# The seam between attention and the routed experts: order of the last masks, weights, gathers and attention groups

## The chip, the cores and the metric

One core of one Trainium2 chip. The metric is device time in microseconds of one execution of the whole program; lower is better. The core's engines run their own instruction streams in order and meet at semaphores: TensorE (PE, matmuls), VectorE (DVE), ScalarE (ACT), GpSimd (POOL, which also issues indirect DMAs) and SyncE (SP, which issues plain DMAs). TensorE's clock has two levels, 1.2 and 2.4 GHz; the trace gives the granted share.

## What is computed

x has 4 x 1024 tokens of 256 numbers. xn is its layer norm. The result is x + attention(xn) + experts(xn):

```python
qkv = xn @ w_attn.T                      # 16 heads of 16
# causal linear attention, phi = elu + 1, chunks of 128 tokens with a carried state
scores = where(mask, q_c @ k_c.T, 0)
num = scores @ v_c + q_c @ S;  den = scores.sum(-1) + q_c @ z
S = S + k_c.T @ v_c;           z = z + k_c.sum()
attn = (num / (den + 1e-6)) @ w_proj.T
# 8 experts, each token goes to the one of the largest gate logit
e = argmax(xn @ gate_w.T + gate_b + expert_bias)
ffn = relu(xn @ w1[e] + b1[e]) @ w2[e] + b2[e]
```

## The kernel before

**Attention.** The 4096 tokens are 32 chunks of 128 (NC = 32; 0 to 31). A loop over steps p runs every engine over several chunks at once, in a software pipeline written out by hand: at step p, for instance, TensorE does qk of chunk p - 1, the scores of chunk p - 3 and the projection of chunk p - 4. Products are taken in split precision: an f16 high part and an f16 remainder. For a chunk c the last steps are: scores(c) (TensorE, L466), s_mask(c, 0..3) (VectorE, L785, causal mask out of PSUM), inter(c) and pv(c) (L479, L495), y1(c) (ScalarE copy, L1186), yt1(c) (transposes, L525), y(c) (VectorE, division, L801 to L807), yt2(c) (L531), y2(c) (ScalarE copy, L1192), pr(c) (projection, L539), res(c) (VectorE adds the residual, L813). SyncE stores [f16 parts of xn | sum] of each chunk to scr (store_res, L346), and the f16 parts alone, earlier, to scr16 (store_x16). Chunks 29, 30 and 31 are finished behind the loop, in a hand-written order on each engine.

**Weights.** Beside attention the experts' weights are brought into f16 high and low parts, 64 quarters (NW = 64, n = 0 to 63) of 128x512. For each: load_split(n) on SyncE (L320) into one of four staging buffers, which it may reuse once p_wlo has counted w_lo(n - 4); w_scale(n) and w_hi(n) on ScalarE (L1207, L1199; split(first, n) does n such pairs); w_lo(n) on GpSimd (L1370). Behind the loop SyncE still issues quarters 58 to 63, GpSimd does w_lo(56), km(31), w_lo(57) to w_lo(62), and w_lo(63) behind the first gather; ScalarE does split(56, 1), vh(31), y1(29), split(57, 3), y1(30), y2(29), split(60, 4), y1(31), y2(30).

**Routing.** Every 8 chunks the picked experts are turned into ranks by a scan and two matmuls, place(g) (L551, L552), which wait for the scan (v_ox) and for vh and lg of the chunks so far. Behind the last, place(3), VectorE does bases (L913 to L919: the first slot of each expert), own, own_sum, own_slot, first_slots (L972 to L977, the slot KT of each token), to_slots (L983, L985) and places (L967), which build one-hot matrices. 32 matmuls (L628) of these make the table ids: for each of 39 slots (NS = 39) of 128 places, all of one expert, the tokens in it. GE, ESF, ESP and PKF (L1051 to L1057) give each slot's expert; v_es releases the register loads of TensorE and VectorE.

**Slots.** Per slot s: a gather of the rows (GpSimd, indirect DMA), tx(s) (transposes, L647, and ScalarE copy, L1264), 8 groups g1(s, f) of 6 matmuls (L682), bias, high and low (L1080, L1273, L1092), 8 groups g2 (L695) 12 groups behind g1 (LAG), rest and add_up (L1100 to L1112), scatter (L1433). The first three slots gather f16 rows from scr16 (gather_x16, L1421), which needs only ids; the others take scr (gather, L1428), which needs the stores of the last chunks, chunk 31's among them. The gathers from scr begin with slot 0's, since its residual is needed too, so slot 3's is the fourth. PE's order around the seam:

```python
scores(NC - 2)
st(NC - 2)
place(3)
...
a.then_inc(t_ids, 1)
e.wait_ge(S["t32"], n_state(NC - 2))
inter(NC - 1)
yt1(NC - 2)
pv(NC - 1)
yt2(NC - 2)
pr(NC - 2)
yt1(NC - 1)
```

yt2(31) and pr(31) stand inside slot 0, after its groups 3 and 5.

Of the kernel before, what the change touches and what calls it, by code (L numbers as in the profile page):

```python
# [9 lines left out]
ALU = mybir.AluOpType  # L10
# [58 lines left out]
def program(nc, x, wall, wp, gb, eb, w1, b1, w2, b2, cst, cst2, cst3, tri, out):  # L69
    ctx = ExitStack()  # L70
    with ctx:
# [189 lines left out]
        def experts(engine, tile, unit, s, n):  # L261
# [34 lines left out]
        v_o16, v_ox, t_rk, v_own, v_es, v_eq, v_ao, t_ids, v_ids, d_c16 = (  # L296
            sem(n) for n in ("v_o16", "v_ox", "t_rk", "v_own", "v_es", "v_eq", "v_ao", "t_ids", "v_ids", "d_c16"))
# [83 lines left out]
        def tensor(e):  # L381
# [229 lines left out]

            scores(NC - 2)
            st(NC - 2)
            place(3)
# [19 lines left out]
            yt2(NC - 2)  # L634
            pr(NC - 2)
            yt1(NC - 1)
# [67 lines left out]
            tx(0)  # L704
            for t in range(8 * NS + LAG):
                s, f = t // 8, t % 8
                if s < NS:
                    g1(s, f)
                    if f == 2 and s + 1 < NS:
                        tx(s + 1)  # L710
                    if f == 4 and s + 1 < NS:
                        expert(s + 1)
                if t == 3:
                    yt2(NC - 1)
                if t == 5:
                    pr(NC - 1)
                if t >= LAG:
                    g2((t - LAG) // 8, (t - LAG) % 8)

        def vector(e):  # L720
# [248 lines left out]
            def first_slots():  # L969

                e.wait_ge(v_wmx, NW)
                e.tensor_tensor(RB8, OA, bm(BAS, NC), ALU.mult).then_inc(dv.up(), 1)  # L972
                e.wait_ge(dv.sem, dv.n)
                e.tensor_reduce(OB, RB8, X_AX, ALU.add).then_inc(dv.up(), 1)
                e.wait_ge(dv.sem, dv.n)
                e.wait_ge(p_pl, 3)
                e.tensor_tensor(KT, KS, OB, ALU.add).then_inc(dv.up(), 1)  # L977

            def to_slots(i):

                c = slice(16 * i, 16 * i + 16)
                e.wait_ge(dv.sem, dv.n)
# [57 lines left out]
            res(NC - 3)  # L1040
            e.wait_ge(t_ids, 1)
# [5 lines left out]
            e.scalar_tensor_tensor(ids[:, :], pid, 2048.0, IDP, ALU.add, ALU.subtract).then_inc(v_ids, 1)  # L1047
            s_mask(NC - 1, 1)
            s_mask(NC - 1, 2)
            s_mask(NC - 1, 3)  # L1050
            e.tensor_tensor(GE, bc(cc(C_SL, 5 * NP), 7), bm(CSF[:, 0:7], 5 * NP), ALU.is_ge).then_inc(dv.up(), 1)  # L1051
            e.wait_ge(dv.sem, dv.n)
            e.tensor_reduce(ESF, GE, X_AX, ALU.add).then_inc(dv.up(), 1)
            e.wait_ge(dv.sem, dv.n)
            e.tensor_tensor(ESP, ESF, cc(C_PK, 5 * NP), ALU.mult).then_inc(dv.up(), 1)
            e.wait_ge(dv.sem, dv.n)
            e.tensor_reduce(PKF, ESP.rearrange("p (j i) -> p j i", i=5), X_AX, ALU.add).then_inc(dv.up(), 1)  # L1057
            e.tensor_copy(es[:, :], ESF[:, 0:NS])
            y(NC - 2)
            e.wait_ge(dv.sem, dv.n)  # L1060
            e.tensor_copy(pk[:, :], PKF).then_inc(v_es, 1)
            scales_ffn()
            y(NC - 1)
            res(NC - 2)
# [50 lines left out]
            for s in range(NS + 2):  # L1115
# [5 lines left out]
                if s == 0:  # L1121
                    res(NC - 1)
                if s >= 2:
                    add_up(s - 2)
                if s < NS:
                    low(2 * s)
                    bias(s, 1)
# [5 lines left out]
        def scalar(e):  # L1133
# [120 lines left out]
            y1(NC - 2)  # L1254
            y2(NC - 3)
            split(NW - 4, 4)
# [19 lines left out]
            y2(NC - 1)  # L1276
            for s in range(NS):
                if s + 1 < NS:
                    tx(s + 1)
                high(2 * s)  # L1280
                high(2 * s + 1)

        def gpsimd(e):
# [129 lines left out]
            for n in range(NW - 7, NW - 1):  # L1413
                w_lo(n)
# [22 lines left out]
            gather_x16(0)  # L1437
            w_lo(NW - 1)
            for s in range(1, NX0):
                gather_x16(s)  # L1440
# [73 lines left out]
```

## Time and profile before

| | |
|---|---|
| median of 3 runs | 518.91 us (518.23 to 519.29) |
| the profiled execution, device time | 517.53 us |
| its span, first to last instruction | 515.7 us |
| TensorE (PE) busy | 487.0 us, 94% |
| VectorE (DVE) busy | 394.5 us, 76% |
| ScalarE (ACT) busy | 278.7 us, 54% |
| GpSimd (POOL) busy | 304.1 us, 59% |
| granted TensorE clock, mean | 0.980 |

Attention fills the first 265 us or so, the slots run from 287.6 us on; between them lies the seam that the change is about. Busy times are of an average over stages. Times in the rows are us from the start of the span. "L" numbers are lines of the kernel. In the timeline a line is start, length, engine, line, operation, and in brackets how long the engine idled before it and for what; consecutive instructions of one kind are merged (x16).

### The profile page before, as it was taken

Reading aid. Unit: us, or ns where it says so; the run is one execution under the profiler, and the core shown is the slowest. Engines: PE = TensorE matmul, PEld = TensorE weight load, DVE = VectorE, ACT = ScalarE, POOL = GpSimd, SP = SyncE. Lnnn points to the kernel's source line nnn. Section 1 sums busy time; section 2 is a strip of 40 time slices with the busy share of each in tenths; the row PEclk is TensorE's granted clock in tenths of the full one; section 3 lists DMA queues with packets and bytes.
Section 4 is the critical chain, followed back from the end, with each engine's and each line's share of the span. In section 5 each row is a group of like instructions: output and inputs, shape, how many; then the busy total and the mean of one; then the engine's idle time right before and its main releaser. Section 6 shows DMA issues by size and latency. Waiting matters only on the chain.

```text
span 515.7 us, 17822 instructions
## 1 busy us (share of the span) xinstructions
PE 487.0 (94%) x6225; PEld 402.9 (78%) x6225; DVE 394.5 (76%) x851; ACT 278.7 (54%) x536; POOL 304.1 (59%) x498
## 2 busy tenths in 40 slices
PE   7799999999999999999966969999999999999996
PEld 6678887888878888788845758888888888888884
DVE  3688888988889888897897446776776776777775
ACT  3458788778787778878863213323333333333330
POOL 5666888788888888888646074344344344343122
PEclk9799999999999999999988889999999999999999
DMA  8716667676576667665533162221222212200000
GB/s 262 244 53 177 198 200 208 194 216 209 187 221 178 213 187 222 205 205 169 182 111 111 65 174 73 63 79 59 73 64 65 82 59 62 72 23 26 23 15 3
DMA packets 39059, 67.50 MB, mean 131 GB/s; under 512 B 6237, under 2 KB 14686, under 8 KB 38848
## 3 DMA queue, kind: packets, MB, share of 16 engines
q1 hardware_dynamic: 33840, 53.37, 33.5%
q0 software_dynamic: 5136, 12.99, 8.5%
q8 instruction: 56, 0.92, 0.7%
q14 instruction: 27, 0.22, 0.2%
HBM read 51.39 MB, written 17.69 MB: 134 GB/s over the span
## 4 chain that ended last, share of the span: by engine, by line
PE 86%; DVE 5%; DMA 3%; issue 2%; ACT 1%; POOL 1%; DVEq 0%; POOLq 0%; ACTq 0%
PE ps L682 20%; PE ps L695 19%; PE ps L424 8%; PE ps L539 6%; PE ps L466 6%; PE ps L495 5%; PE ps L479 4%; PE ps L442 4%; PE ps L509 3%; PE ps L525 2%; PE ps L647 2%; PE ps L449 2%; PE ps L531 1%; DMA XR<-scr,AR 1%; PE ps L407 1%
## 5 line engine op out<-in xcount | busy, mean ns | idle before, releaser
L682 PEld LDWEIGHTS ps<-AR,W 128*128 x1872 | 131.5, 98 | 41.1 <-issue 2.0
L682 PE MATMUL ps<-AR,W 128*128 128x128 f16 x1872 | 156.1, 220 | 0.9 <-ACT AR L1264 0.9
L695 PE MATMUL ps<-W,ST 128*128 x624 | 151.4, 328 | 0.0
L1273 ACT ACTIVATE ST<-ST 128x512 f16<-128x512 f32 x78 | 49.2, 630 | 117.4 <-DVE ST L1080 117.4
L1080 DVE SCALAR_TENSOR_TENSOR ST<-ps,TAs,B1S 128x512 f32<-128x512 f32 x78 | 58.6, 751 | 48.5 <-PE ps L682 48.5
L1433 POOL DMA_INDIRECT out<-AR x39 | 39.6, 1015 | 93.9 <-DVE AR L1112 90.6
L785 DVE TENSOR_TENSOR AR<-ps,CT 128x512 f32<-128x512 f32 x128 | 82.0, 683 | 2.0 <-PE ps L466 1.7
L1370 POOL TENSOR_TENSOR W<-ST,W 128x512 f16<-128x512 f32 x64 | 75.1, 1174 | 12.3 <-ACT W L1199 12.0
L1428 POOL DMA_INDIRECT XR<-scr,AR x39 | 44.9, 1151 | 52.6 <-DVE AR L1100 23.8
L1092 DVE SCALAR_TENSOR_TENSOR ST<-ST 128x512 f16<-128x512 f32 x78 | 53.6, 687 | 14.9 <-ACT ST L1273 14.9
L424 PE MATMUL ps<-xT,WA 128*128 128x128 f16 x768 | 49.5, 222 | 3.2 <-ACT xT L1148 3.2
L695 PEld LDWEIGHTS ps<-W,ST 128*128 128x128 f16 x624 | 48.5, 98 | 1.6
L424 PEld LDWEIGHTS ps<-xT,WA 128*128 128x128 f16 x768 | 45.6, 99 | 4.5 <-ACT xT L1148 4.2
L1207 ACT ACTIVATE ST<-ST,SC 128x512 f32<-128x512 f32 x64 | 46.4, 725 | 0.0
L820 DVE TENSOR_REDUCE MX<-ST 128x1 f32<-128x512 f32 x64 | 42.5, 665 | 0.1
L1199 ACT ACTIVATE W<-ST 128x512 f16<-128x512 f32 x64 | 40.4, 631 | 1.1
L1322 POOL TENSOR_SCALAR AR<-XR,mv,rsn 128x256 f32<-128x256 f32 x32 | 39.8, 1243 | 1.7
L1264 ACT ACTIVATE AR<-ps 128x512 f16<-128x512 f16 x39 | 23.3, 596 | 31.9 <-PE ps L647 31.9
L1336 POOL TENSOR_TENSOR AR<-AR,CT 128x512 f32<-128x512 f32 x32 | 33.3, 1040 | 7.6 <-DVE AR L779 7.4
L539 PE MATMUL ps<-AR 128*128 128x256 f32 x128 | 36.8, 412 | 0.9 <-ACT AR L1192 0.9
L466 PE MATMUL ps<-AR 32*128 32x256 f32 x512 | 36.8, 401 | 0.9 <-DVE XR L813 0.9
L495 PE MATMUL ps<-AR 128*32 128x128 f32 x1024 | 34.8, 276 | 0.6 <-DVE AR L785 0.6
(149 smaller groups left out, 786.5 us busy)
## 6 DMA issues: line engine op xcount, KB each, us to landing
ST<-in_w SPq DMA_DIRECT2D x128, 256.0 KB, 4.3
scr<-XR SPq DMA_DIRECT2D x32, 256.0 KB, 2.1
XR<-in_x SPq DMA_DIRECT2D x32, 128.0 KB, 4.7
scr<-XR SPq DMA_DIRECT2D x32, 128.0 KB, 4.5
AR<-in_b SPq DMA_DIRECT2D x1, 1024.0 KB, 5.1
AR<-in_wall SPq DMA_DIRECT2D x2, 388.0 KB, 3.8
XR<-scr,AR POOLq DMA_INDIRECT x40, 3.6
out<-AR POOLq DMA_INDIRECT x39, 2.5
```

The source lines that it names most:

```text
L424: a = e.matmul(PS[0][:, j * 128:(j + 1) * 128], WA[:, wl, k, j * 128:(j + 1) * 128], x_part(c, xl_, k), start=(n == 1), stop=(n == 6))
L466: a = e.matmul(psc(c, r)[:, g * 256:(g + 1) * 256], QK[c % 2][rows, 256 + g * 128:384 + g * 128], QM[c % 2][rows, g], start=True, stop=True)
L495: a = e.matmul(PS[5][32 * b:32 * b + 32, j * 128:(j + 1) * 128], V32[c % 2][:, 8 * g + 4 * i + b, :], S32[2 * i + t][:, (2 * g + o) * 128: ...
L539: a = e.matmul(py(c)[:, 256:512], YT2[:, k * 128:(k + 1) * 128], WPF[:, k, :], start=(k == 0), stop=(k == 1))
L682: a = e.matmul(dst, W[:, off:off + 57472][:, bass.ds(place_of(s), 128)], XT16[s % 2][:, xl * 256 + k * 128:xl * 256 + (k + 1) * 128], star ...
L695: a = e.matmul(PS[4 + s % 2][:, 0:w], src[h % 4][:, fs], W[:, off:off + 57344 + w][:, bass.ds(place_of(s), w)], start=(f == 0 and w == 512 ...
L785: e.tensor_tensor(S32[r].rearrange("p (b n) -> p b n", b=4), psc(c, r)[:, :].rearrange("p (b n) -> p b n", b=4), msk, ALU.mult).then_inc(s ...
L1080: e.scalar_tensor_tensor(H32[h % 2].rearrange("p (f n) -> p f n", f=4), PS[h % 4][:, :].rearrange("p (f n) -> p f n", f=4), TAs[:, :, 0][: ...
L1092: e.scalar_tensor_tensor(HL2[h % 4], H32[h % 2], 0.0, HH[h % 4], ALU.max, ALU.subtract).then_inc(v_hl, 1)
L1207: e.activation(src, src, ACT.Copy, scale=SC[:, n // 8, n % 8 // 4:n % 8 // 4 + 1].bitcast(F32)).then_inc(a_wsc, 1)
L1273: e.activation(HH[h % 4], H32[h % 2], ACT.Relu).then_inc(a_hh, 1)
L1370: e.tensor_tensor(lo_, src, hi, ALU.subtract).then_inc(p_wlo, 1)
```

## The change

- TensorE: place(3) moves ahead of scores(30) and st(30). yt2(30), pr(30) and yt1(31) move from ahead of the first slot to inside slot 0: behind tx(0), behind group 0 and behind group 1. yt2(31) and pr(31) go from behind groups 3 and 5 to behind groups 4 and 6.
- VectorE: KT counts on a semaphore of its own, v_kt. The first three operations of the slots' experts (GE, ESF, ESP) move ahead of the wait for the table, the rest right behind ids, so v_es comes ahead of three of chunk 31's masks and y(30). res(30) goes ahead of y(31); res(31) goes behind low(0).
- ScalarE: quarters 60 and 61 are split ahead of y2(29), 62 and 63 behind it. y2(31) goes behind tx(1).
- GpSimd: a wait for v_kt ahead of w_lo(57); w_lo(63) ahead of the first gather.

```diff
@@ -293,8 +293,8 @@
         v_mx, t_mx, v_mm, t_mxa, v_sc, v_ffn = (sem(n) for n in ("v_mx", "t_mx", "v_mm", "t_mxa", "v_sc", "v_ffn"))
 
         p_tt, p_carry, v_ro, p_pl = (sem(n) for n in ("p_tt", "p_carry", "v_ro", "p_pl"))
-        v_o16, v_ox, t_rk, v_own, v_es, v_eq, v_ao, t_ids, v_ids, d_c16 = (
-            sem(n) for n in ("v_o16", "v_ox", "t_rk", "v_own", "v_es", "v_eq", "v_ao", "t_ids", "v_ids", "d_c16"))
+        v_o16, v_ox, t_rk, v_own, v_es, v_kt, v_eq, v_ao, t_ids, v_ids, d_c16 = (
+            sem(n) for n in ("v_o16", "v_ox", "t_rk", "v_own", "v_es", "v_kt", "v_eq", "v_ao", "t_ids", "v_ids", "d_c16"))
 
         v_rb, t_tx, a_tx, v_out, t_g2 = (sem(f"f_{n}") for n in ("rb", "ptx", "tx", "out", "g2"))
 
@@ -609,9 +609,9 @@
                     e.transpose(PBX, BM[:, :], ID32).then_inc(t_bmx, 1)
 
 
+            place(3)
             scores(NC - 2)
             st(NC - 2)
-            place(3)
             yt1(NC - 3)
             inter(NC - 2)
             pv(NC - 2)
@@ -631,9 +631,6 @@
             inter(NC - 1)
             yt1(NC - 2)
             pv(NC - 1)
-            yt2(NC - 2)
-            pr(NC - 2)
-            yt1(NC - 1)
 
             def tx(s):
 
@@ -702,6 +699,7 @@
             e.wait_ge(v_es, 1)
             expert(0)
             tx(0)
+            yt2(NC - 2)
             for t in range(8 * NS + LAG):
                 s, f = t // 8, t % 8
                 if s < NS:
@@ -710,9 +708,13 @@
                         tx(s + 1)
                     if f == 4 and s + 1 < NS:
                         expert(s + 1)
-                if t == 3:
+                if t == 0:
+                    pr(NC - 2)
+                if t == 1:
+                    yt1(NC - 1)
+                if t == 4:
                     yt2(NC - 1)
-                if t == 5:
+                if t == 6:
                     pr(NC - 1)
                 if t >= LAG:
                     g2((t - LAG) // 8, (t - LAG) % 8)
@@ -974,12 +976,12 @@
                 e.tensor_reduce(OB, RB8, X_AX, ALU.add).then_inc(dv.up(), 1)
                 e.wait_ge(dv.sem, dv.n)
                 e.wait_ge(p_pl, 3)
-                e.tensor_tensor(KT, KS, OB, ALU.add).then_inc(dv.up(), 1)
+                e.tensor_tensor(KT, KS, OB, ALU.add).then_inc(v_kt, 1)
+                e.wait_ge(v_kt, 1)
 
             def to_slots(i):
 
                 c = slice(16 * i, 16 * i + 16)
-                e.wait_ge(dv.sem, dv.n)
                 e.tensor_tensor(EQS[:, :, c], SLX[:, :, c], bm(KT[:, c], NS), ALU.is_equal).then_inc(dv.up(), 1)
                 e.wait_ge(dv.sem, dv.n)
                 e.tensor_tensor(EQS[:, :, c], EQS[:, :, c], bm(IDX[:, c], NS), ALU.mult).then_inc(v_eq, 1)
@@ -1038,6 +1040,11 @@
             places(3)
             s_mask(NC - 1, 0)
             res(NC - 3)
+            e.tensor_tensor(GE, bc(cc(C_SL, 5 * NP), 7), bm(CSF[:, 0:7], 5 * NP), ALU.is_ge).then_inc(dv.up(), 1)
+            e.wait_ge(dv.sem, dv.n)
+            e.tensor_reduce(ESF, GE, X_AX, ALU.add).then_inc(dv.up(), 1)
+            e.wait_ge(dv.sem, dv.n)
+            e.tensor_tensor(ESP, ESF, cc(C_PK, 5 * NP), ALU.mult).then_inc(dv.up(), 1)
             e.wait_ge(t_ids, 1)
             pid = PS[1][:, 0:NS]
             e.tensor_scalar(IDZ, pid, 0.0, 2048.0, ALU.is_equal, ALU.mult).then_inc(dv.up(), 1)
@@ -1045,23 +1052,17 @@
             e.scalar_tensor_tensor(IDP, pid, 0.0, IDZ, ALU.is_gt, ALU.subtract).then_inc(dv.up(), 1)
             e.wait_ge(dv.sem, dv.n)
             e.scalar_tensor_tensor(ids[:, :], pid, 2048.0, IDP, ALU.add, ALU.subtract).then_inc(v_ids, 1)
+            e.tensor_reduce(PKF, ESP.rearrange("p (j i) -> p j i", i=5), X_AX, ALU.add).then_inc(dv.up(), 1)
+            e.tensor_copy(es[:, :], ESF[:, 0:NS])
+            e.wait_ge(dv.sem, dv.n)
+            e.tensor_copy(pk[:, :], PKF).then_inc(v_es, 1)
             s_mask(NC - 1, 1)
             s_mask(NC - 1, 2)
             s_mask(NC - 1, 3)
-            e.tensor_tensor(GE, bc(cc(C_SL, 5 * NP), 7), bm(CSF[:, 0:7], 5 * NP), ALU.is_ge).then_inc(dv.up(), 1)
-            e.wait_ge(dv.sem, dv.n)
-            e.tensor_reduce(ESF, GE, X_AX, ALU.add).then_inc(dv.up(), 1)
-            e.wait_ge(dv.sem, dv.n)
-            e.tensor_tensor(ESP, ESF, cc(C_PK, 5 * NP), ALU.mult).then_inc(dv.up(), 1)
-            e.wait_ge(dv.sem, dv.n)
-            e.tensor_reduce(PKF, ESP.rearrange("p (j i) -> p j i", i=5), X_AX, ALU.add).then_inc(dv.up(), 1)
-            e.tensor_copy(es[:, :], ESF[:, 0:NS])
             y(NC - 2)
-            e.wait_ge(dv.sem, dv.n)
-            e.tensor_copy(pk[:, :], PKF).then_inc(v_es, 1)
             scales_ffn()
+            res(NC - 2)
             y(NC - 1)
-            res(NC - 2)
 
             at = {}
 
@@ -1118,12 +1119,13 @@
                         e.wait_ge(v_es, 1)
                     expert(s)
                     bias(s, 0)
-                if s == 0:
-                    res(NC - 1)
                 if s >= 2:
                     add_up(s - 2)
                 if s < NS:
                     low(2 * s)
+                if s == 0:
+                    res(NC - 1)
+                if s < NS:
                     bias(s, 1)
                 if 1 <= s <= NS:
                     rest(s - 1)
@@ -1252,8 +1254,9 @@
             y1(NC - 3)
             split(NW - 7, 3)
             y1(NC - 2)
+            split(NW - 4, 2)
             y2(NC - 3)
-            split(NW - 4, 4)
+            split(NW - 2, 2)
             y1(NC - 1)
             y2(NC - 2)
 
@@ -1273,10 +1276,11 @@
                 e.activation(HH[h % 4], H32[h % 2], ACT.Relu).then_inc(a_hh, 1)
 
             tx(0)
-            y2(NC - 1)
             for s in range(NS):
                 if s + 1 < NS:
                     tx(s + 1)
+                if s == 0:
+                    y2(NC - 1)
                 high(2 * s)
                 high(2 * s + 1)
 
@@ -1410,7 +1414,8 @@
             e.wait_ge(v_ox, 4)
             w_lo(NW - 8)
             km(NC - 1)
-            for n in range(NW - 7, NW - 1):
+            e.wait_ge(v_kt, 1)
+            for n in range(NW - 7, NW):
                 w_lo(n)
             e.wait_ge(S["xt"], NC)
             for c in range(NC - R, NC):
@@ -1434,9 +1439,7 @@
                                      bounds_check=NT - 1, oob_is_err=False).then_inc(d_sca[s % 3], 16)
 
             e.wait_ge(v_ids, 1)
-            gather_x16(0)
-            w_lo(NW - 1)
-            for s in range(1, NX0):
+            for s in range(NX0):
                 gather_x16(s)
             for c in range(NC - R, NC):
                 e.wait_ge(d_scr[c % R], 16 * (c // R + 1))
```

## Rows read from the trace of the kernel before

**Rows 1.** The chain of waits from 235 us on: start us, length us, what.

```profile
268.92 2.07 PE ps L539 x4
271.00 2.93 PE ps L385 x30
273.93 2.32 PE ps L628 x32
...
292.31 2.00 DMA scr<-XR
...
299.46 3.66 DMA XR<-scr,AR
...
306.03 0.64 PE ps L682 x6
308.18 0.34 PE ps L682 x6
```

**Rows 2.** Windows: us, busy us of each engine, TensorE's granted clock, DMA share, GB/s.

```profile
269.00:270.00 1.00, 1.00 (x3) 0.82 (x4) 0.96 (x3) 0.97 (x2) 0.00 (x0) 0.50 0.00 0
```

**Rows 3.** The timeline from 254.5 to 277 us, all engines.

```profile
258.84 0.46 ACT L1175 ACTIVATE AR<-ps,SV 128x256 f32<-128x256 f32 x1
...
258.91 1.15 PE L466 MATMUL ps<-AR 32*128 32x256 f32 x16 [0.91 <-DVE XR L813]
...
260.59 0.27 PE L552 MATMUL ps<-AR,tri 128*128 128x64 bf16 x1
...
261.19 3.65 POOL L1370 TENSOR_TENSOR W<-ST,W 128x512 f16<-128x512 f32 x3
...
263.09 0.51 DVE L915 TENSOR_SCALAR AR<-AR 128x8 f32<-128x8 f32 x1
...
263.84 1.02 DVE L919 TENSOR_TENSOR AR<-AR 128x8 bf16<-128x8 f32 x1
...
266.68 0.19 DVE L977 TENSOR_TENSOR AR<-AR 128x32 f16<-128x32 f32 x1
...
268.49 0.38 ACT L1192 ACTIVATE AR<-ps 128x256 f32<-128x256 f32 x1 [4.38 <-PE ps L531]
...
268.77 0.71 ACT L1207 ACTIVATE ST<-ST,SC 128x512 f32<-128x512 f32 x1
...
270.04 2.25 DVE L967 TENSOR_TENSOR XR<-ST,AR 128x1024 f16<-128x1024 f16 x2
270.05 0.70 ACT L1207 ACTIVATE ST<-ST,SC 128x512 f32<-128x512 f32 x1
```

**Rows 4.** DMA landings: quarters loaded from 259 us on (L320); the first gather (L1421).

```profile
DMA to landing us min/median/max: 2.7/3.0/3.2
...
DMA to landing us min/median/max: 3.0/3.0/3.0
```

**Rows 5.** The timeline from 277 us to slot 3's transpose, all engines.

```profile
276.85 1.88 DVE L785 TENSOR_TENSOR AR<-ps,CT 128x512 f32<-128x512 f32 x3
...
277.93 1.26 POOL L1421 DMA_INDIRECT XR<-scr,AR  x1 [3.49 <-DVE AR L1047]
...
282.15 0.42 DVE L807 TENSOR_TENSOR AR<-ps,DN 128x256 f32<-128x256 f32 x1
...
283.54 1.92 PE L539 MATMUL ps<-AR 128*128 128x256 f32 x4 [0.47 <-ACT AR L1192]
...
285.25 1.06 PE L525 MATMUL ps<-CT,AR 128*128 128x128 f32 x4
...
286.77 0.60 ACT L1264 ACTIVATE AR<-ps 128x512 f16<-128x512 f16 x1 [3.29 <-PE ps L647]
...
287.61 1.61 PE L682 MATMUL ps<-AR,W 128*128 128x128 f16 x18 [0.88 <-ACT AR L1264]
...
291.86 0.42 DVE L813 TENSOR_TENSOR XR<-ps,XR 128x256 f32<-128x256 f32 x1 [1.05 <-PE ps L539]
...
303.17 0.40 PE L647 MATMUL ps<-id,XR 128*128 128x128 f16 x4 [4.31 <-DMA XR<-scr,AR]
```

## The prediction

> **What bounds the kernel now.** I read the chain of waits first. In its last 212 us it is TensorE alone, one slot after another; the last piece in it that is not TensorE is the landing of a gathered row block at 303.1 us [rows 1]. That is the gather for slot 3, the first slot whose transpose reads scr and not scr16. TensorE had run dry at 298.85 and stood 4.31 us until 303.17 [rows 5]. So the end moves one for one with the moment at which slot 3's rows land, as long as TensorE is dry by then. Going back: the gathers wait for the store of chunk 31's sum (issued 292.31, 2.00 us to land), and that for res(31), which ends at 291.86 + 0.42 = 292.28 [rows 1, 5]. From res(31) to the transpose of slot 3 nothing is touched by the change: 303.17 - 291.86 = 11.3 us, of which the fourth gather (issued 299.46, 3.66 us) is the tail.
>
> Ahead of res(31) stand two stretches. The first ends with the routing table: y2(29) on ScalarE at 268.49 [rows 3], pr(29), 30 warm matmuls and the 32 matmuls that invert the order, until 276.25 [rows 1]. The second goes from there to the first expert matmul at 287.61 and to res(31). The windows show TensorE at a granted 0.50, its 1.2 GHz level, in the first [rows 2], and pr, the same two products in both, takes 2.07 us in the first and 1.92 in the second [rows 1, 5], so the second is slow as well. What the level is worth: a group of six expert matmuls takes 0.64 us at 1.2 GHz against 0.34 at 2.4 GHz [rows 1]. I take half of pr's and yt1's rows as their price at 2.4 GHz.
>
> **Part 1: place(3) ahead of scores(30).** scores(30) began at 258.91. place(3) waits for all of vh, and vh(31) on ScalarE ends only at 258.84 + 0.46 = 259.30 [rows 3]. So place(3) can start at 259.3 and, with its weight load, takes about 0.4 (its last matmul is 0.27), and scores(30) starts 0.75 us later. VectorE takes the masks right behind scores(30) and comes to bases only after them, at 262.9, when the old place(3) (over at 260.86) had long been done. So this edit gains nothing and costs 0.75. Bounds: 0.4 (TensorE's queue overlaps) to 0.9.
>
> **Part 2: GpSimd waits for v_kt.** In bases, the operation at L915 took 0.51 and L919 took 1.02 us, and the latter ended with w_lo(59) (three w_lo from 261.19 for 3.65); a like-sized operation with GpSimd silent takes 0.19 (L977) [rows 3]. Without GpSimd beside them the two lose 0.3 + 0.85 = about 1.2. KT was written at 266.68 + 0.19 = 266.87; it is now written at 266.87 + 0.75 - 1.2 = **266.4**. Bounds 265.7 to 266.9.
>
> What is queued behind that wait decides the case. w_lo(57) frees the staging buffer into which quarter 61 is loaded (load_split(61) on SP waits for p_wlo 58). Before, w_lo(57) was over at 262.4. Now it starts at 266.45 and ends at 267.6 (3.65 / 3, with the spacing, 1.2). Loads of quarters land 2.7 to 3.2 us after issue, median 3.0 [rows 4]: quarter 61 is there at 270.7. Quarters 62 and 63 come 1.2 us apart behind it.
>
> **Part 3: ScalarE's split(60, 2) ahead of y2(29).** Quarter 60 is loaded in time and is a gain in an idle stretch. Quarter 61 is not: ScalarE, in order, waits for it until 270.7, then scales and copies it (one pair is 270.05 - 268.77 = 1.28 us [rows 3]), and does y2(29) at **272.0** instead of 268.49: **+3.5 us**. Lower bound: 265.7 + 1.2 + 2.7 + 1.28 = 270.9, +2.4. Upper: 266.9 + 1.3 + 3.4 + 1.28 = 272.9, +4.4. yt2(29) has run long before; nobody else can do pr(29), and warm and the table stand behind it in TensorE's order. pr, warm and table took 2.07 + 2.93 + 2.32 = 7.3. TensorE now stands from about 268 to 272, and is at 1.2 GHz when it starts again, as before; I take 0.2 off, since it is then busy without a break and the table's part at 2.4 GHz may be longer than before. The table is done at 276.25 + 3.3 = **279.55**.
>
> Beside it: after KT, to_slots and places (seven operations with two SBUF inputs) now run beside four w_lo back to back, where only the last two places did (2.25 us for the pair, some 0.9 too much [rows 3]). At 0.45 each that is 3 us: places(3) ends at about 266.4 + 4.5 + 3 = 274, ahead of the table's start (about 277). Cost nothing, covered by pr and warm. The Trainium skill, page SBUF — State Buffer, on DVE against GpSimd, says that with two SBUF inputs on VectorE and a reading GpSimd operation the second to start blocks fully until the first ends. By that rule the wait is bounded by the w_lo there are: below 4.8 us, and places(3) would end by 275.8, still under cover.
>
> The three operations GE, ESF and ESP move ahead of the table, behind res(29), into VectorE's wait for warm and table, 2.93 + 2.32 us [rows 1]: nothing. With that cover gone v_es would come later by their length, as it does before. Behind the table PKF and two casts remain, 0.7 by the row of L977; v_es comes at about 281.0. w_lo(63) moves ahead of the first gather; ScalarE is through quarter 63 at about 275, so it ends at 276.2, before the table: nothing.
>
> **Part 4: the last groups inside slot 0.** From the end of the table to the first gather's row is 277.93 - 276.25 = 1.7 us, to its landing another 3.0 [rows 4, 5]: 279.55 + 4.7 = 284.25. VectorE meanwhile: ids, the casts until 281.0, three masks (1.88) to 282.9, y(30) to 283.8 (its last operation is 0.42, the two small ones before it as much again [rows 5]); pv(31) ends some 0.7 behind the masks. So tx(0) runs at 284.25, then yt2(30): six transposes, 1.1 at 1.2 GHz by yt1's four, which took 1.06. ScalarE does y2(30) first, then the copy of tx(0), 0.3 + 0.6 [rows 5]; 0.25 later the first expert matmul: 284.25 + 1.1 + 0.05 + 0.9 + 0.25 = **286.6**, against 287.61. Of the 3.3 us lost, 4.3 are bought back, mostly by pr(30) (1.92) and yt1(31) (1.06), which stood ahead of it.
>
> But res(31) needs these just the same. From the first expert matmul to pr(31)'s end TensorE now has seven groups g1, pr(30), yt1(31), tx(1), yt2(31), pr(31): at 2.4 GHz 7 x 0.34 + 1.0 + 0.5 + 0.2 + 0.2 + 1.0 = 5.3 us. It begins at 1.2 GHz and, as in the two stretches before, stays so for some 3 to 4 us: plus 1.8, 7.1. VectorE takes res(31) now behind low(0), which waits for y2(31) and high(0) on ScalarE: 0.3. res(31) starts at 286.6 + 7.4 = **294.0** against 291.86: **+2.1**. Bounds of this part: full clock at once 5.4 (-2.0), low throughout 10 (+2.6, unlikely).
>
> TensorE's own work until it is dry again ends near 300.8, slot 3 lands at 305.3, so it is dry 4.5 us, again, and the clock falls again (0.64 for a group at 306.03 [rows 1]). Nothing of it is gained back.
>
> **Sum.** v_kt -0.45; w_lo, load, split before y2(29): +3.95; clock -0.2; head of slot 0 -4.3; inside slot 0 +3.1: +2.1. Span 515.7 + 2.1 = 517.8; the profiled execution took 517.53, which is 1.4 below the median of the runs, 518.91. On the median: **520.9 us** (+0.4%).
>
> **Rivals.**
> A. *Faster.* The groups taken out of the way of slot 0 buy more than the late copy costs. Mechanism: TensorE keeps 2.4 GHz from slot 0's start, so that part 4 takes 5.4 and not 7.4, and y2(29) is at its lower bound (+2.4). Then res(31) is 2.1 - 2.0 - 1.1 = 1.0 us earlier: 517.9. If quarter 61 did not hold up y2(29) at all (1.6 us behind KT as before), it would be 3.9 less than that forecast, -1.8: 517.1. At the forecast's clock this side is reached where y2(29) starts before 268.9, with the full clock before 270.9. Against it: p_wlo 58 is a hard condition, and no load here landed in under 2.7. For it: no row fixes where in slot 0 the clock will rise.
> B. *No change* (within 0.2%, 1.04 us, about what a measurement of this kernel can tell from no change). The same mechanisms, half of each: y2(29) +2.9, 1 us less at 1.2 GHz in slot 0: 519.5.
> C. *The masks bound the table.* By the skill's rule of the lock, if the waits also push w_lo and thereby the loads of 62 and 63, or if each of the seven operations waits a whole w_lo (7 x 1.2 = 8.4), places(3) ends at 279.3, 2 us behind TensorE, and the forecast becomes 523. The only pair in the trace lost 0.9 in two, so this is unlikely.
> D. *The clock stays low after slot 3's stall or through slot 0*: +1 to 2.5 on the forecast, 522 to 523.4.
>
> **How the numbers follow.** Forecast's case 0.56, A 0.11, B 0.19, C 0.05, D 0.09. Slower by over 0.2%: 0.56 + 0.05 + 0.09 = 0.70; same 0.19; faster 0.11. Forecast's own range, from the bounds of part 3 (-1.1, +0.9) and of the clock (-1, +1): 519.5 to 522.3. To hold 8 in 10 it takes in B and most of D: 518.5 to 523.2. A below that and the far end of C and D are left out.
>
> **What would show it.** (1) scores(30) starts near 259.7, behind place(3). (2) L915 and L919 near 0.2 us each, KT about 0.5 earlier. (3) w_lo(57) behind KT, and ScalarE idle before the scaling of quarter 61, with a DMA as its releaser; y2(29) near 272. (4) The table's end near 279.5. (5) First expert matmul 286 to 287, res(31) near 294, and the same 4 to 5 us of dry TensorE before slot 3. The prediction is wrong if y2(29) starts before 270, or if TensorE isn't dry before slot 3: then the slots, not the gather, set the end, and the earlier slot 0 counts in full.

## The result, and the profile after

The changed kernel is slower. Over 13 runs each it took 519.98 us against 517.53 us, the ratio is 1.0051 (95% interval 1.0036 to 1.0066), which is 2.6 us (1.9 to 3.4). The forecast was 520.9 us, or +2.0 on the three runs of the kernel before that it started from. The runs of the kernel before that stood beside the experiments have spans from 514.5 to 517.9 us, on average 515.6 where the mean granted clock was 0.986 and 517.0 where it was 0.977, so that one profiled execution can stand 1 to 2 us off the median of its kernel. The profiled execution took 519.57 us, its span is 517.8 us, against 515.7 before. From the page of the changed kernel, the span, TensorE's busy time and the row of its granted clock:

```profile
span 517.8 us, 17824 instructions
...
PE 486.3 (94%) x6225; PEld 403.2 (78%) x6225; DVE 395.3 (76%) x851; ACT 278.8 (54%) x536; POOL 304.4 (59%) x498
...
PEclk9899999999999999999988879999999999999999
```

TensorE is busy as long as before; what was added is idle time. It lies where the seam is. The timeline of the changed kernel from 259 to 279 us (line numbers have moved by a few: L917, L921, L979 here are L915, L919, L977 of before, L985 and L987 are to_slots, L969 is places, L1374 w_lo, L1209 the scaling of a quarter, L1194 y2):

```profile
259.32 0.19 PE L551 MATMUL ps<-AR,one 128*128 128x72 bf16 x1 [1.39 <-DVE AR L910]
...
259.81 1.15 PE L466 MATMUL ps<-AR 32*128 32x256 f32 x16 [0.20 <-issue]
...
263.99 0.17 DVE L917 TENSOR_SCALAR AR<-AR 128x8 f32<-128x8 f32 x1
...
264.40 0.17 DVE L921 TENSOR_TENSOR AR<-AR 128x8 bf16<-128x8 f32 x1
...
266.39 0.19 DVE L979 TENSOR_TENSOR AR<-AR 128x32 f16<-128x32 f32 x1
...
266.66 5.41 POOL L1374 TENSOR_TENSOR W<-ST,W 128x512 f16<-128x512 f32 x4 [5.51 <-DVE AR L979]
...
268.18 1.32 DVE L987 TENSOR_TENSOR ST<-ST 128x624 f16<-128x624 f16 x1
269.42 1.63 DVE L969 TENSOR_TENSOR XR<-ST,AR 128x1024 f16<-128x1024 f16 x1
270.80 0.72 ACT L1209 ACTIVATE ST<-ST,SC 128x512 f32<-128x512 f32 x1 [4.53 <-DMA ST<-in_w]
...
272.09 0.36 ACT L1194 ACTIVATE AR<-ps 128x256 f32<-128x256 f32 x1
...
272.51 2.08 PE L539 MATMUL ps<-AR 128*128 128x256 f32 x4 [4.48 <-ACT AR L1194]
...
273.69 2.24 DVE L969 TENSOR_TENSOR XR<-ST,AR 128x1024 f16<-128x1024 f16 x2
...
276.70 2.48 PE L628 MATMUL ps<-ST,XR 128*128 128x39 f16 x32
```

Against [rows 3]: place(3) now waits until 259.32, and the scores follow at 259.81 instead of 258.91. L917 and L921 take 0.17 each instead of 0.51 and 1.02. KT (L979) is written at 266.58 instead of 266.87. w_lo(57) to w_lo(59), which before stood ahead of KT, now begin behind it, and w_lo(60), whose quarter is now split early, follows them at once (x4). ScalarE comes to quarter 61 at 270.80 only; the bracket names a DMA into the staging buffer and 4.53 us of idle time. y2(29) follows at 272.09 (268.49 before), pr(29) 0.4 behind it, the table at 276.70 to 279.2 (276.25 before). Note also the durations of the one-hot operations (to_slots and places), 1.32 to 1.63 us each in these rows and 2.24 for a pair: they come up again.

The same timeline further on, to the transpose of slot 3:

```profile
284.39 0.38 PE L644 MATMUL ps<-id,XR 128*128 128x128 f16 x4 [1.61 <-DMA XR<-scr,AR]
...
286.15 0.82 PE L679 MATMUL ps<-AR,W 128*128 128x128 f16 x6 [1.15 <-ACT AR L1267]
...
286.76 2.02 PE L539 MATMUL ps<-AR 128*128 128x256 f32 x4
...
293.66 0.42 DVE L815 TENSOR_TENSOR XR<-ps,XR 128x256 f32<-128x256 f32 x1
...
304.65 0.61 PE L644 MATMUL ps<-id,XR 128*128 128x128 f16 x4 [4.93 <-DMA XR<-scr,AR]
```

Against [rows 5]: tx(0) 284.39, the first expert matmul 286.15 (287.61), res(31) 293.66 (291.86), slot 3's transpose 304.65 (303.17), and TensorE is dry, which is to say idle for want of rows, for 4.93 us ahead of it (4.31). The chain of waits, behind slot 3's start:

```profile
309.10 0.64 PE ps L692 x2
...
312.50 0.34 PE ps L679 x6
```

A group still takes 0.64 at 309.1; before, it was back at 0.34 at 308.18 [rows 1]. From slot 3's transpose to the end are 213.2 us for 212.5. So 1.5 us stand at slot 3, and the rest of the 2.1 us of span goes with the longer stretch at 1.2 GHz behind it.

### The profile page after: what moved, and what is told of

Read it like the earlier page. It is cut to its first block, busy times and chain, and to the rows that moved or that the text cites. A ratio compares the mean times of both kernels' runs of the same rounds, so it can differ in the third digit from the quotient of the medians.

```text
span 517.8 us, 17824 instructions
## 1 busy us (share of the span) xinstructions
PE 486.3 (94%) x6225; PEld 403.2 (78%) x6225; DVE 395.3 (76%) x851; ACT 278.8 (54%) x536; POOL 304.4 (59%) x498
## 4 chain that ended last, share of the span: by engine, by line
PE 85%; DVE 4%; issue 4%; POOL 3%; DMA 3%; ACT 2%; DVEq 0%; POOLq 0%; ACTq 0%
PE ps L692 19%; PE ps L679 19%; PE ps L424 8%; PE ps L539 6%; PE ps L466 6%; PE ps L495 5%; PE ps L479 4%; PE ps L442 4%; PE ps L509 3%; PE ps L525 2%; PE ps L644 2%; PE ps L449 1%; DMA XR<-scr,AR 1%; PE ps L531 1%; PE ps L407 1%
## 5 line engine op out<-in xcount | busy, mean ns | idle before, releaser
L1374 POOL TENSOR_TENSOR W<-ST,W 128x512 f16<-128x512 f32 x64 | 76.0, 1190 | 12.8 <-ACT W L1201 7.1
L1093 DVE SCALAR_TENSOR_TENSOR ST<-ST 128x512 f16<-128x512 f32 x78 | 53.6, 687 | 15.6 <-ACT ST L1276 15.6
L1209 ACT ACTIVATE ST<-ST,SC 128x512 f32<-128x512 f32 x64 | 46.4, 725 | 4.5 <-DMA ST<-in_w 4.5
```

The costliest lines, as they stand in the source:

```text
L1093: e.scalar_tensor_tensor(HL2[h % 4], H32[h % 2], 0.0, HH[h % 4], ALU.max, ALU.subtract).then_inc(v_hl, 1)
L1209: e.activation(src, src, ACT.Copy, scale=SC[:, n // 8, n % 8 // 4:n % 8 // 4 + 1].bitcast(F32)).then_inc(a_wsc, 1)
L1374: e.tensor_tensor(lo_, src, hi, ALU.subtract).then_inc(p_wlo, 1)
```

## The experiments

All times are medians; the kernel before ran beside each group of four on the same chip (517.53, 517.8 and 518.2 us in the three groups). The ratios are to it, with 95% intervals; where two runs are compared, it is by their ratios, and such a difference is uncertain by about 1 us.

**Run 1: the split undone.** In the changed kernel:

```diff
-            split(NW - 4, 2)
             y2(NC - 3)
-            split(NW - 2, 2)
+            split(NW - 4, 4)
```

> The changed kernel with one thing undone: ScalarE does y2(29) first and quarters 60 to 63 behind it. Theory (quarter 61, late by the wait for v_kt, holds up y2(29), 3.3 of the changed kernel's loss): y2(29) goes from 272.1 to about 268.2, the table's end from 279.2 to about 276.1 (the one-hot masks, slowed by the four w_lo beside them, end near 275.5 and may bind it by some 0.2), res(31) near 290.2. Time about 3.1 us below the changed kernel and 1 to 2 us below the kernel before: 516. Rival (the loss lies in the masks, which run beside w_lo): the table's end stays within 1 us of 279.2 and the time within 1 us of the changed kernel, 519.5. Rival (the groups inside slot 0 lose): time at the kernel before or above, 517.5 to 518.5.

Measured: 519.33 us, ratio 1.0039 (1.0022 to 1.0055). Against the changed kernel that is some 0.6 us and not 3.1: the theory as it stood falls, and both signs of the first rival (table's end and time within 1 us of the changed kernel's) are met. TensorE's timeline of this run:

```profile
260.19 1.88 PE L466 MATMUL ps<-AR 32*128 32x256 f32 x16 [0.19 <-issue]
...
274.39 1.31 PE L628 MATMUL ps<-ST,XR 128*128 128x39 f16 x16
...
278.62 0.78 PE L628 MATMUL ps<-ST,XR 128*128 128x39 f16 x8 [0.73 <-DVE XR L969]
```

Two things are to be seen. The first half of the table's 32 matmuls ran at 274.39, right behind the warm ones; the last eight ran at 278.62, after a wait for the last one-hot matrix. y2(29) was early (269.68), and nothing came of it: a second wait stood right behind the first. And scores took 1.88 us instead of 1.15, behind the longer idle stretch ahead of the moved place(3) (1.40 us, 0.91 before): the clock had fallen. KT was written at 268.19 in this execution.

**Run 2: the wait undone.**

```diff
-            e.wait_ge(v_kt, 1)
             for n in range(NW - 7, NW):
```

> The changed kernel with one thing undone: GpSimd doesn't wait for v_kt. Theory: w_lo(57) is over at 262.4 again, quarter 61 is loaded at 265.4, y2(29) waits for y(29) alone. KT is written at 267.7 (0.8 late by place(3), with bases slowed as before), y2(29) at 269.3, the table's end at 277.0, res(31) near 291.2: 0.5 to 1 us below the kernel before, 516.8, and 2.5 below the changed one. Rival (the split ahead of y2(29) costs by itself, ScalarE being busy with it): y2(29) later than 270, time within 1 us of the changed kernel.

Measured: 518.80 us, ratio 1.0018 (1.0001 to 1.0036). In its profile y2(29) starts at 270.52, waiting for y(29) and no longer for a quarter; KT is as late as 269.03, 2.45 us later than in the changed kernel. Two rows of this run say why, the second of them TensorE's granted clock (0.50, against 1.00 in the changed kernel) from 262 to 264 us:

```profile
267.85 1.18 DVE L979 TENSOR_TENSOR AR<-AR 128x32 f16<-128x32 f32 x1
```

```profile
262.00:264.00 2.00, 2.00 (x11) 2.00 (x11) 1.70 (x3) 1.70 (x3) 1.83 (x3) 0.50 0.37 121
```

The write of KT ran into a w_lo and took 1.0 us longer than with GpSimd silent (0.19), and here too the clock had fallen behind the moved place(3): scores(31) starts 5.73 us behind scores(30), for 4.46 in the changed kernel, 1.3 us lost. The wait is worth some 1.7 us of the changed kernel's loss. The expected gain over the kernel before did not come; these two are why in this execution. y2(29) is later than 270, as the rival had it, but not because ScalarE was busy: it waited for y(29).

**Run 3: the wait and the split alone**, in the kernel before:

```diff
+            split(NW - 4, 2)
             y2(NC - 3)
-            split(NW - 4, 4)
+            split(NW - 2, 2)
...
+            e.wait_ge(v_kt, 1)
             for n in range(NW - 7, NW - 1):
```

> The kernel before with two things of the change: GpSimd's wait for v_kt ahead of w_lo(57), and quarters 60 and 61 split ahead of y2(29). Theory: KT at 265.7 (bases undisturbed, place(3) where it was), w_lo(57) to 266.9, quarter 61 loaded at 269.9, y2(29) at 271.2 against 268.49; nothing buys it back, so the table's end, the first expert matmul and the end come 2.7 us later: 520.2. Rival (the loss of the changed kernel comes from the groups moved into slot 0): within 1 us of the kernel before.

Measured: 520.74 us, ratio 1.0068 (1.0046 to 1.0091), +3.5 us. y2(29) at 271.05 (expected 271.2). So these two together make a loss as large as the changed kernel's, without the groups in slot 0 and without place(3).

**Run 4: the part around slot 0 alone** (the changed kernel with its place(3), its wait and its split undone):

> The changed kernel without its place(3), its wait for v_kt and its split: what is left is the part around slot 0 (attention's last groups inside slot 0, the experts' numbers ahead of the table, w_lo(63) ahead of the first gather). Theory: the table's end stays at 276.3, tx(0) runs at 281, the first expert matmul at about 283.2 instead of 287.6, res(31) at 290.1 instead of 291.9 (13.8 behind the table's end, since the attention groups are now inside): 1.8 us below the kernel before, 515.7. Rival (moving them gains nothing since res(31) needs them all the same): within 0.7 us of the kernel before.

Measured: 516.94 us, ratio 0.9991 (0.9978 to 1.0005). The shape is as expected in the trace (table's end 275.2, first expert matmul 282.34, res(31) 289.79, span 514.3), but over the runs only 0.5 us are left of 1.8, and the interval takes in no change. It is the lowest median of all the kernels here; the profiled execution, at 516.06 us, was the fastest of its twelve.

**Run 5: place(3) back.**

```diff
-            place(3)
             scores(NC - 2)
             st(NC - 2)
+            place(3)
```

> The changed kernel with place(3) behind scores(30) and st(30) again. Theory (place(3) ahead of the scores costs 0.9, since it waits for vh(31) and the scores wait behind it): the masks begin near 260.1 again, KT at 265.5, y2(29) at 271.2, the table's end at 278.3, res(31) at 292.8: 0.9 us below the changed kernel. In the run with the split undone the clock also fell to 1.2 GHz right behind the late place(3) (scores took 1.88 us), which the shorter idle stretch may spare: up to 1 us more. Time 518 to 519. Rival (the place is free, as place(3) is needed by bases anyway): same as the changed kernel, 520.

Measured: 520.64 us, ratio 1.0042 (1.0026 to 1.0059). KT at 265.35 and y2(29) at 270.88, as expected. The ratio is 0.5 us below the changed kernel's, within the intervals, and the median is above the 518 to 519 of the theory: in time it can't tell the theory from its rival.

**Run 6: place(3) alone**, the same edit the other way, in the kernel before.

> The kernel before with place(3) ahead of scores(30) and st(30), nothing else. Theory: KT, y2(29), the table and the end 0.9 us later, 518.4; where the clock falls behind the longer idle stretch, up to 2.5 us later. Rival: same as the kernel before.

Measured: 518.37 us, ratio 1.0004 (0.9991 to 1.0017). KT 267.53 against 266.87. A cost of up to 0.9 us is inside the interval, and so is none: inconclusive in time. In the trace KT is late, but the end of the table is not (275.92 against 276.25): pr(29) took 1.13 us instead of 2.07, at the full clock.

**Run 7: the wait and the part around slot 0** (place(3) and the split as before). It asks what the wait costs where the split can't be at fault.

> The part around slot 0 and GpSimd's wait for v_kt; place(3) and the split as before. It asks what the wait costs by itself, through the one-hot operations that then run beside w_lo. Theory after the first four runs (each of these operations waits for a whole w_lo, as in the changed kernel, where the last ended 9.5 us behind KT against 5.6 before): KT 265.5, the last of them ends at 275 to 276, behind the warm matmuls (272.5), so that it binds the table: the table's end 275.7 to 276.7 instead of 275.2 in the run without the wait, time 0.5 to 1.5 us above that run: 517.5 to 518.5. Rival (as predicted: some 0.45 each, covered by pr and warm): table's end at 274.8 from y2(29) at 267.1, time 0.4 us below that run, 516.5.

Measured: 518.87 us, ratio 1.0016 (1.0002 to 1.0030); against run 4, 1.3 us more. The timeline of this run:

```profile
265.89 0.19 DVE L979 TENSOR_TENSOR AR<-AR 128x32 f16<-128x32 f32 x1
...
267.57 0.38 ACT L1194 ACTIVATE AR<-ps 128x256 f32<-128x256 f32 x1 [3.04 <-PE ps L531]
...
268.94 1.64 DVE L969 TENSOR_TENSOR XR<-ST,AR 128x1024 f16<-128x1024 f16 x1
...
272.21 1.31 PE L628 MATMUL ps<-ST,XR 128*128 128x39 f16 x16
...
273.23 3.21 DVE L969 TENSOR_TENSOR XR<-ST,AR 128x1024 f16<-128x1024 f16 x2
...
276.50 0.77 PE L628 MATMUL ps<-ST,XR 128*128 128x39 f16 x8 [0.74 <-DVE XR L969]
```

y2(29) starts 1.5 us behind KT (1.6 in the kernel before). The one-hot operations end at 273.23 + 3.21 = 276.44, 10.4 us behind KT, and the last eight matmuls of the table wait for them. This is the cost of the wait by itself, and it is not nothing.

**Run 8: slot 3's gather first**, on run 4's kernel. It tests the prediction's first paragraph, that the end moves with the landing of slot 3's rows.

```diff
-            for s in range(NG):
+            for s in (3, 0, 1, 2, 4, 5, 6, 7):
```

> The part around slot 0 alone (as in an earlier run), and GpSimd gathers slot 3's rows from scr first, then those of slots 0, 1, 2, 4 to 7. Theory (the end goes with the landing of slot 3's rows while TensorE is dry before it, 5.05 us in that run): slot 3's rows are issued three gathers of 1.3 us earlier, so TensorE is dry for about 1.1 us, and may keep its clock: 3.9 to 5.5 us below that run, 511.5 to 513. Rival (the slots are bound by something else, as by the residuals of slots 0 to 2, which land 1.3 us later each): less than 1.5 us below that run, above 515.5.

Measured: 518.46 us, ratio 1.0009 (0.9997 to 1.0021), 0.9 us slower than run 4 and not 4 faster. TensorE's waits from 293 to 312 us, in run 4:

```profile
PE ps L644 <- DMA XR<-scr,AR: 5.0, 1, 5.0
```

and in this run:

```profile
PE ps L679 <- issue: 3.8, 6, 1.2
PE ps L692 <- issue: 1.1, 3, 0.5
PE ps L644 <- DMA XR<-scr,AR: 0.5, 1, 0.5
```

and some of its timeline (all engines):

```profile
298.15 0.40 PE L644 MATMUL ps<-id,XR 128*128 128x128 f16 x4 [0.48 <-DMA XR<-scr,AR]
...
302.82 0.99 POOL L1431 DMA_INDIRECT XR<-scr,AR  x1 [0.30 <-issue]
303.50 0.33 PE L679 MATMUL ps<-AR,W 128*128 128x128 f16 x3 [1.23 <-issue]
...
304.12 1.00 POOL L1431 DMA_INDIRECT XR<-scr,AR  x1 [0.30 <-issue]
```

The wait for the rows is gone (0.48 us), slot 3's transpose is at 298.15. But from 300 us on TensorE gets its instructions in small bits, one to three matmuls every 0.7 us, until shortly behind the last gather in the row (306.4). Idle time of 4.9 us is back, in pieces named issue (TensorE waits for nothing that the profile shows). The pieces also end inside a group of six matmuls, where the kernel has no wait, so it is not the residuals of slots 0 to 2 that TensorE waits for; by its number (above 515.5 us) the rival had it right, its cause is not what the trace shows.

**Run 9: the gathers paced**, on run 8's kernel:

```diff
             for s in (3, 0, 1, 2, 4, 5, 6, 7):
-                if s == NG - 1:
-                    e.wait_ge(t_tx, 1)
+                if s >= 5:
+                    e.wait_ge(t_tx, s - 1)
```

> The part around slot 0 alone, slot 3's gather first, and the gathers of slots 5, 6 and 7 each held back until the transpose of slot 3, 4 and 5. With slot 3's gather first and all eight in a row, TensorE had its rows at 298.15 but then stood in short stretches put down to issue until 307.8, while the gathers ran. Theory (the burst of gathers slows TensorE's supply of instructions): with fewer in flight these stretches shrink to 2 us or less, and the time falls 2 to 4 us below that run, to 513.5 to 516. Rival (the stretches are due to something else, as to the registers of slot 2's instructions): they stay at 5 us and more, time at 517.5 to 518.5.

Measured: 519.44 us, ratio 1.0026 (1.0005 to 1.0048). TensorE's waits from 293 to 330 us, and its timeline where they are longest:

```profile
PE ps L679 <- issue: 2.9, 3, 1.2
PE ps L692 <- issue: 1.6, 2, 1.1
PE ps L644 <- issue: 1.5, 2, 1.1
PE ps L644 <- DMA XR<-scr,AR: 0.6, 1, 0.6
```

```profile
318.20 0.33 PE L644 MATMUL ps<-id,XR 128*128 128x128 f16 x3 [1.10 <-issue]
...
322.49 0.27 PE L679 MATMUL ps<-AR,W 128*128 128x128 f16 x1 [1.20 <-issue]
323.89 0.26 PE L679 MATMUL ps<-AR,W 128*128 128x128 f16 x1 [1.12 <-issue]
```

The pieces did not shrink, they moved (in an execution of 521.83 us, one of the three slowest of twelve, which lie between 517.07 and 522.21): one near 302, and most between 317 and 324, where GpSimd, held back before, issued gathers and scatters one behind the other without a break (312.5 to 322.8). Their sum, 6.0 us, is what the rival forecast, but they follow the indirect DMAs and not slot 2's instructions, so its cause falls. The expected gain does not come all the same: the DMAs have to be issued at some time.

**Run 10: the kernel before, paced.**

> The kernel before with the same order and pace of the gathers and nothing of the change. Theory: slot 3's rows land at 299.3 instead of 303.1, 2 to 4 us below the kernel before, 513.5 to 515.5. Rival (the end isn't set by slot 3's landing but by the sum of TensorE's work): same as before, 517.5.

Measured: 521.78 us, ratio 1.0067 (1.0044 to 1.0090): 3.5 us slower, with 5.5 us of such waits. The theory that the landing of slot 3 alone sets the end falls here as well, and so does the rival, which had no change.

**Run 11: the one-hot operations without w_lo**, on run 9's kernel:

```diff
-            for n in range(NW - 7, NW):
+            for n in range(NW - 7, NW - 4):
                 w_lo(n)
+            e.wait_ge(v_ao, 4)
+            for n in range(NW - 4, NW):
+                w_lo(n)
...
-            warm(30)
+            warm(12)
```

> The paced kernel with w_lo(60) to w_lo(63) behind the last one-hot operation, and 12 warm matmuls instead of 30 ahead of the table. It asks whether these operations lose their length to w_lo. Theory: without w_lo beside them the seven end 4.5 us behind KT (5.6 before, 9.5 in the changed kernel). They end at about 271, TensorE comes out of pr and 12 warm matmuls at about 272: the table ends 0 to 1.5 us earlier than in the paced kernel (the clock may stay low in it and take that back). Time 0 to 1 us below the paced kernel. Rival (they are slow by themselves): they still end 5.5 us or more behind KT.

Measured: 519.43 us, ratio 1.0020 (1.0003 to 1.0037). Its timeline:

```profile
266.22 0.19 DVE L979 TENSOR_TENSOR AR<-AR 128x32 f16<-128x32 f32 x1
...
267.79 0.48 DVE L987 TENSOR_TENSOR ST<-ST 128x624 f16<-128x624 f16 x1
...
268.19 0.69 DVE L969 TENSOR_TENSOR XR<-ST,AR 128x1024 f16<-128x1024 f16 x1
...
269.71 1.28 DVE L969 TENSOR_TENSOR XR<-ST,AR 128x1024 f16<-128x1024 f16 x2
...
271.07 4.78 POOL L1373 TENSOR_TENSOR W<-ST,W 128x512 f16<-128x512 f32 x4 [6.69 <-ACT W L1201]
```

With GpSimd silent the same operations take 0.48 and 0.64 to 0.69 us, and they end at 270.99, 4.6 us behind KT. The table ends 8.0 us behind KT (run 9: 9.9). So the operations lose their length to w_lo, and the rival falls. But the 1.9 us by which the table is nearer to KT come from the other edit: in run 9 the one-hot operations had ended (272.72) ahead of the table's start (274.41), and the warm matmuls take 1.49 us here for 3.41. In time it is level with run 9 over the runs. In the two profiled executions the way from KT's write to the end is 1.0 us shorter (252.0 us for 253.1); where the rest went stays open.

**Run 12: the changed kernel, paced.**

> The changed kernel with the same order and pace of the gathers. Theory: its late table stays, so that it loses against the paced kernel what it loses now, 3 us, and gains on itself as much as the kernel before does: 515.5 to 518. Rival (the dry stretch hid part of the loss): more than 4 us above the paced kernel.

Measured: 522.74 us, ratio 1.0083 (1.0056 to 1.0109): 3 us above run 9, as expected, so the rival falls; but there is no gain on itself (515.5 to 518 was expected), pacing costs it 1.7 us.

## Why the prediction was right, point by point

**Part 1, place(3).** Scores at 259.81 (259.7 forecast), masks 0.9 later. Its price in time, 0.75 in the sum (as part of v_kt's -0.45), is 0.5 us by run 5 and 0.2 by run 6, neither clear of its interval. The runs showed a risk the prediction did not have: TensorE is idle 1.40 us ahead of the moved place(3), and the clock can fall behind that. Of the five profiled executions with place(3) moved it fell in three (runs 1, 2 and 12; granted 0.53, 0.50 and 0.50 from 262 to 264 us), and scores(31) came 1.2 to 1.4 us later for it; with place(3) in its old place the granted clock was 1.00 from 258 to 266 us in all nine. The changed kernel's profile is one of the two that were spared.

**Part 2, the wait.** The gain in bases came as stated (1.53 to 0.34 us for the two operations) and KT is at 266.58 (266.4 forecast). w_lo(57) began at 266.66, quarter 61 was there at 270.80 (270.7).

**Part 3, the split.** y2(29) at 272.09 (272.0), table's end 279.2 (279.55). The chain went as worked out, piece by piece. The step that failed is the sentence that to_slots and places beside four w_lo cost "nothing, covered by pr and warm". They ended at 275.93, 9.35 us behind KT, where with GpSimd silent they end 4.6 behind it (run 11): 4.8 us lost, not 3. In the changed kernel this was covered by 0.8 us only, and only because y2(29) was late. So rival C was no remote case but a second limit right behind the first: run 1 took away the late copy (3.3 us of lateness) and got 0.6 us; run 7 against run 5, the same edit without place(3), got 1.3. In the order of the runs the changed kernel's +2.6 us are made of: the part around slot 0 -0.5 (run 4), the wait +1.3 (run 7), the split on top of it +1.3 (run 5), place(3) +0.5 (the changed kernel), each with an uncertainty of about 1 us. The forecast's sum had the whole loss on the split (+3.95) and a gain on the wait (-0.45); by the runs the two cost 1.3 us each. The distance from the write of KT to the table's end says much the same without the runs' spread. The wait adds 2.5 us to it (run 7 against run 4) and brings KT 1.2 us forward (6.75 us behind the start of scores(30) for 7.96), which leaves 1.3; the split adds 1.9 (run 5 against run 7):

| kernel | KT to table's end, us | what ends last ahead of the table |
|---|---|---|
| before | 9.5 | warm, behind pr(29) |
| run 4 | 8.9 | warm |
| run 2: split, place(3) | 9.9 | warm |
| run 7: wait | 11.4 | one-hot operations |
| run 1: wait, place(3) | 11.4 | one-hot operations |
| run 3: wait, split | 13.3 | y2(29) behind quarter 61 |
| run 5: wait, split | 13.2 | y2(29) behind quarter 61 |
| after: wait, split, place(3) | 12.8 | y2(29) behind quarter 61 |
| run 11: no w_lo beside the one-hot operations, 12 warm matmuls | 8.0 | warm |

(From the start of KT's write to the end of the last table matmul. "Warm" are the matmuls on a constant that stand ahead of the table. How far KT itself moved is not in it. All but the kernel before and run 3 have the part around slot 0.)

The size was wrong because it was taken as a mean over a pair (0.9 us too much for two, 0.45 each). The pair's first had run free: it began at 270.04, ahead of the w_lo at 270.22, and the whole 0.9 was on the second. In the changed kernel, against run 11, one of the seven operations was held by 0.2 us, five by 0.8 to 1.0 each, and one, the first of the last pair, ran free; that makes the 4.8. The Trainium skill, page SBUF — State Buffer, section Summary: rules for kernel authors, has the rule that of a VectorE operation with two SBUF inputs and a GpSimd operation that reads SBUF the second to issue blocks fully until the first ends. The trace agrees: each of the five ended 0.3 or 0.5 us behind the w_lo that was running when it began. The prediction's bound by that rule, 4.8 us, was reckoned from four w_lo; the operations were held by w_lo(57) to w_lo(62), so that it met the measured loss to the tenth is luck.

**Part 4, the groups in slot 0.** First expert matmul 286.15 (286.6), res(31) 293.66 (294.0), table's end to res(31) 14.5 us (14.45 forecast, 15.6 before; 14.6 in runs 4 and 5). The head of slot 0, from the table's end to the first expert matmul, took 7.0 us for 11.4 and gave back 4.4 (4.3 forecast), and the inside of it took 3.3 more (3.1).

**The end.** Slot 3 at 304.65 (305.3), dry 4.93 us (4.5), span 517.8 (517.8). That it agrees to the tenth is partly luck: res(31) was 0.3 early, the clock came back later behind slot 3, and in this execution it did not fall behind place(3). Over the runs the loss was 2.6 us and not 2.0; the time of 519.98 us lies below the 520.9 of the forecast because the three runs of the kernel before from which it started (518.91) were 1.4 us above the median of its thirteen.

**What the prediction said that is not so.** The last sentence had it that, were TensorE not dry before slot 3, an earlier slot 0 would count in full. Runs 8 to 10 and 12 took the dry stretch away and were 0.9 to 3.5 us slower than the same kernels with it. The wait for the rows was there, but it was not what an earlier landing would save: with it gone, TensorE is short of instructions while the indirect DMAs are issued one behind the other. That the dry stretch had hidden this is a reading; the same row of gathers ran in the kernel before, from 295.15 to 307.55, and TensorE, working again from 303.17 on, had no such stand. "One for one with slot 3's landing" holds only with the order of the gathers kept: from slot 3's transpose to the end are 212.5 us before, 213.2 after, 213.4 in run 4, but 220.0 in run 8. Two small slips of its arithmetic changed nothing: rival B's terms, 0.6 and 1.0 us less than the forecast, give 519.3 and not 519.5, and the load of 3.4 us in the upper bound of part 3 is above the 3.2 of its rows.

The parts of the loss, 0.5 to 1.3 us each, are no larger than the spread between executions of one kernel, and each profile is one execution.

## What to carry to other kernels

When a copy or a load is moved ahead of a piece of the critical chain, look for what frees its buffer, on every queue, and for what has just been made to wait there: two edits can meet in one buffer. (The split without the wait was run only together with place(3), in run 2; the wait without the split cost 1.3 us, for another reason.) Ask of every wait that is found what is second: here three limits stood within a few microseconds (the late copy, the one-hot operations, TensorE's own chain), and taking away the first, 3.3 us, bought 0.6 to 1.3. And for operations of VectorE with two SBUF inputs beside GpSimd operations back to back, take nearly the whole length of GpSimd's operation as the price of each (0.8 to 1.0 us beside a w_lo of 1.16 us here), not a mean over a pair of which one ran free.

## What the runs showed of the hardware

In runs 8 to 12, while GpSimd issued indirect DMAs without a break (1.0 us each, 1.3 apart), TensorE got new instructions only in bits: one to three matmuls every 0.7 us in run 8, with stands of up to 1.2 us put down to issue, 4.9 to 6.3 us in sum. In the kernel before, the changed one and runs 1 to 7 there is none of it from 293 to 330 us, though GpSimd issues a like row of gathers; there TensorE had stood idle for the rows of slot 3. What TensorE and the indirect DMAs share no run here shows. That the code itself came late does not show either: from 300.5 to 308 us, around the stands of run 8, no packet of the instruction queue was under way, and none in the kernel before, which had no stands; from 317 to 324 us there is one in run 9, which stands, and one in run 4 and the kernel before, which don't.

A VectorE operation with two SBUF inputs that began beside a w_lo ended behind it: to_slots took 1.32 to 1.44 us instead of 0.48, places 1.6 instead of 0.69, the write of KT 1.18 instead of 0.19 (run 2). The w_lo beside them grew too, from 1.16 us to 1.39 to 1.60. Two kinds with one SBUF input were held as well: the f32 operation at L915 of the kernel before (0.51 instead of 0.17) and a cast to int32 in run 11 (0.91 instead of 0.17). Operations that read PSUM (a mask, 0.68 beside a w_lo and alone) and a reduction (0.45 both ways) were not slowed.

TensorE's granted clock was 1.00 up to the end of an idle stretch of 1.40 us in run 1 and 0.50 from 261 to 263 us, right behind it:

```profile
260.00:261.00 1.00, 0.81 (x11) 0.84 (x15) 0.00 (x0) 0.97 (x3) 1.00 (x2) 0.73 0.66 242
261.00:262.00 1.00, 1.00 (x13) 0.35 (x5) 0.00 (x0) 0.97 (x3) 0.53 (x1) 0.50 0.40 90
```

In the changed kernel's profile the same stretch of 1.39 us was followed by no fall (1.00 throughout). Three of five executions with this stretch had the fall; what decides it was not found.
